# Linear attention: query sums halved by GpSimd, key copies on ScalarE, query round 1 earlier

## The reference

```python
# b = 32 images, C = 32 channels, n = 256 positions, heads = 4, dh = 32
xn = x / norm * g[None, :, None, None] * C ** 0.5
q, k, v = jnp.split(einsum('bchw,oc->bohw', xn, w_qkv), 3, axis=1)
k = concatenate([mk, k], axis=-1)      # 4 memory keys per head
v = concatenate([mv, v], axis=-1)      # and their values
q = softmax(q, axis=-2) * scale        # over the 32 channels of a head
k = softmax(k, axis=-1)                # over the positions
context = einsum('bhdn,bhen->bhde', k, v)
out = einsum('bhde,bhdn->bhen', context, q)
return einsum('bchw,oc->bohw', out, w_out) + b_out
```

## Time and profile before

| | us |
|---|---|
| median of 3 runs | 586.63 |
| lowest and highest | 584.84, 587.69 |
| profiled execution, its own time | 583.12 |
| its span | 581.3 |
| end of the linear attention stage in it | 84.41 |
| VectorE busy, whole span | 408.9 (70%) |
| TensorE busy, whole span | 504.9 (87%) |
| GpSimd busy, whole span | 158.7 (27%) |
| mean granted TensorE clock | 0.966 of full speed |

### The profile page before, as it was taken

How to read it: one execution, slowest core, us unless ns; L and a number is a source line. 1 busy time by engine, 2 the same in 40 slices (tenths; PEclk the granted TensorE clock), 3 DMA queues, 4 the chain that set the end, 5 groups by cost and what they waited for, 6 DMA issues and landing times. The chain is left out here.

```text
span 581.3 us, 15235 instructions
## 1 busy us (share of the span) xinstructions
PE 504.9 (87%) x6330; PEld 289.8 (50%) x6337; DVE 408.9 (70%) x766; ACT 303.6 (52%) x525; POOL 158.7 (27%) x210
## 2 busy tenths in 40 slices
PE   7856889998897989798898888899999999999993
PEld 3445654466655642365555534436543654365420
DVE  5669977775454799787889838866756584658463
ACT  3257544234342310359888844465656555656482
POOL 0116422000000000405666600002860386038500
PEclk9989899999999889999999979979999999999997
DMA  8400015000000381000000000000000000000002
GB/s 257 44 8 3 3 35 206 1 1 2 1 2 1 69 200 23 2 1 1 3 1 2 3 19 2 7 12 3 1 3 11 1 2 1 12 1 2 1 7 77
DMA packets 22560, 15.03 MB, mean 26 GB/s; under 512 B 17465, under 2 KB 20569, under 8 KB 22362
## 3 DMA queue, kind: packets, MB, share of 16 engines
q1 hardware_dynamic: 22490, 14.00, 9.7%
HBM read 8.71 MB, written 1.08 MB: 17 GB/s over the span
## 5 line engine op out<-in xcount | busy, mean ns | idle before, releaser
L2030 ACT ACTIVATE R<-ps 128x512 f32<-128x512 f32 x96 | 52.1, 594 | 41.5 <-PE ps L1743 41.5
L2205 DVE TENSOR_REDUCE R<-ps 128x4 f32<-128x1024 f32 x48 | 56.6, 1210 | 10.0 <-PE ps L1729 9.5
L2113 POOL TENSOR_TENSOR R<-R 128x512 f32<-128x512 f32 x42 | 53.3, 1268 | 15.3 <-ACT R L2030 15.2
L1519 POOL TENSOR_TENSOR R<-R 128x512 f32<-128x512 f32 x32 | 45.3, 1417 | 43.2 <-DVE R L1453 43.2
L1453 DVE TENSOR_TENSOR R<-ps,lasting 128x512 f32<-128x512 f32 x64 | 41.2, 685 | 11.7 <-PE ps L1379 11.7
L1743 PE MATMUL ps<-tmpA,R 32*128 32x256 f32 x384 | 49.3, 374 | 0.0
L1729 PE MATMUL ps<-R,tmpA 32*128 32x256 f32 x384 | 47.7, 400 | 0.0
L1486 ACT ACTIVATE R<-R 128x1536 f32<-128x1536 f32 x32 | 47.3, 1479 | 0.1
L1379 PE MATMUL ps<-R,Q 32*128 32x128 f32 (+1 forms) x512 | 29.9, 346 | 10.0 <-ACT R L1502 10.0
L1743 PEld LDWEIGHTS ps<-tmpA,R 32*128 32x128 f32 x384 | 36.2, 185 | 1.0
L1379 PEld LDWEIGHTS ps<-R,Q 32*128 32x128 f32 x512 | 23.9, 184 | 20.8 <-DVE R L1453 16.9
(11 more groups left out here) (323 smaller groups left out, 1082.9 us busy)
## 6 DMA issues: line engine op xcount, KB each, us to landing
R<-z SPq DMA_DIRECT2D x32, 128.0 KB, 2.4
R<-in_qv SPq DMA_DIRECT2D x1, 2560.0 KB
x<-in_x SPq DMA_DIRECT2D x4, 256.0 KB, 3.5
out<-x SPq DMA_DIRECT2D x4, 256.0 KB, 3.9
lasting<-in_lasting SPq DMA_DIRECT2D x1, 811.0 KB, 8.5
early<-in_early SPq DMA_DIRECT2D x1, 793.5 KB, 7.6
scatter<-in_scatter SPq DMA_DIRECT2D x1, 512.0 KB, 6.2
P<-scratch_w SPq DMA_DIRECT2D x16, 32.0 KB, 2.5
```

The lines of the kernel that those rows point to most:

```text
L1519: pool.tensor_tensor(diagonal(u), diagonal(u), diagonal(u), ALU.mult).then_inc(diag_squared[1], 1)
L2030: act.activation(m.et[:, g % 2, j, :], ps[:, turned_bank(g, j), :], ACT.Exp)\
L2113: pool.tensor_tensor(m.esum[:, g % 2, two, :], m.et[:, g % 2, two, 0:N], m.et[:, g % 2, two, N:2 * N], ALU.add).then_inc(sg["halves_added" ...
L2205: dve.tensor_reduce(m.parts[:, g % 2, :, a:a + 2, 3 * g].rearrange("p s i -> p i s"), ps[:, a:a + 2, :].rearrange("p i (s m) -> p i s m", ...
```

## The change

Four parts. The sums: GpSimd adds the upper 16 channels of each head to the lower 16 (`add_halves`, 128x256) into two alternating buffers in `m.z`, and VectorE's sum reads 16 instead of 32 values per head. GpSimd's list becomes: halves of unit u + 1, then the multiply of unit u. The copies: the turned key maxima and the memory term are copied by ScalarE instead of VectorE; the turning of the memory exponentials and its copy move ahead, beside the weight products of bank 7. TensorE's order: query round 1 goes ahead of key round 0, query round 2 ahead of key round 1, query round 3 from behind context(4, 8) to behind context(0, 4). The lists of VectorE and ScalarE follow: the sums of a round are taken one round later.

```diff
--- before.py
+++ after.py
@@ -216,8 +216,6 @@
     ones_set = sem("la_ones_set")
     memmax_ready = sem("la_memmax_ready")
     memexp_done = sem("la_memexp_done")
-    mem_ready = sem("la_mem_ready")
-    mem_copied = sem("la_mem_copied")
     w2mem_ready = sem("la_w2mem_ready")
     w2mem_copied = sem("la_w2mem_copied")
     kproj_ready = sem("la_kproj_ready")
@@ -236,6 +234,7 @@
     qmax_ready = sem("la_qmax_ready")
     qsub_done = sem("la_qsub_done")
     qexp_done = sem("la_qexp_done")
+    qhalves_added = sem("la_qhalves_added")
     qsum_ready = sem("la_qsum_ready")
     qinv_ready = sem("la_qinv_ready")
     qnorm_done = sem("la_qnorm_done")
@@ -271,6 +270,10 @@
 
     def q_stat(t, u):
         return t[:, 16 * u:16 * u + 16]
+
+    def q_halves(u):
+        at = 768 + u % 2 * 256
+        return m.z[:, at:at + 256].rearrange("p (j h d) -> p j h d", j=J, h=HEADS)
 
     BY_V = (11, 13, 15)
 
@@ -390,12 +393,14 @@
                     key_maxima(J * r + i)
 
             key_maxima_round(0)
+            pe.wait_ge(memexp_done, 1)
             pe.wait_ge(wo_spread, 1)
+            pe.transpose(ps[0:MEM, 7, 256:384], m.kem[:, :], m.ident[:, :])
             pe.matmul(ps[:, 7, 0:128], m.wvt[:, :], m.wobd[:, :], start=True, stop=True)
             pe.matmul(ps[0:MEM, 7, 128:256], m.memvt[:, :], m.wobd[:, :], start=True, stop=True).then_inc(wvo_ready, 1)
             pe.wait_ge(m.lasting_loaded, 16 * 2)
             key_maxima_round(1)
-            pe.wait_ge(wvo_made, 2)
+            pe.wait_ge(wvo_made, 3)
             value_round(0)
             key_maxima_round(2)
             key_maxima_round(3)
@@ -404,24 +409,21 @@
             query_round(0)
             value_round(2)
             value_round(3)
+            query_round(1)
             pe.wait_ge(parts, 4)
             pe.wait_ge(v_copied, UN)
             pe.transpose(ps[:, 4, 0:64].bitcast(BF16), m.kparts[:, :, :].rearrange("p j r -> p (j r)"),
                          m.identb[:, :]).then_inc(turned, 1)
-            pe.wait_ge(memexp_done, 1)
-            pe.transpose(ps[0:MEM, 5, 0:128], m.kem[:, :], m.ident[:, :]).then_inc(mem_ready, 1)
-            pe.wait_ge(mem_copied, 1)
             for h in range(HEADS):
-                mm = pe.matmul(ps[rows_of(h), 6, 0:33], m.kemt[:, rows_of(h)], m.memvo[:, h, :],
+                mm = pe.matmul(ps[rows_of(h), 5, 0:33], m.kemt[:, rows_of(h)], m.memvo[:, h, :],
                                start=True, stop=True)
             mm.then_inc(w2mem_ready, 1)
             pe.wait_ge(turned_copied, 1)
             pe.wait_ge(w2mem_copied, 1)
             key_round(0)
-            query_round(1)
+            query_round(2)
             key_round(1)
             key_round(2)
-            query_round(2)
             key_round(3)
             pe.wait_ge(ones_set, 1)
             pe.wait_ge(kexp_done, 2 * NCH)
@@ -429,7 +431,7 @@
             for u in range(0, 4):
                 query_transposes(u)
                 context(4 * u, 4 * u + 4)
-                if u == 1:
+                if u == 0:
                     query_round(3)
             for u in range(4, 8):
                 query_transposes(u)
@@ -491,6 +493,7 @@
                     dve.tensor_scalar(m.wvo[:, :], ps[:, 7, 0:128], m.gs[:, 0:1], None, ALU.mult).then_inc(wvo_made, 1)
                     dve.tensor_copy(m.memvo[:, :, 0:C], ps[0:MEM, 7, 128:256].rearrange("p (h c) -> p h c", h=HEADS))\
                         .then_inc(wvo_made, 1)
+                    dve.tensor_copy(m.kemt[:, :], ps[0:MEM, 7, 256:384]).then_inc(wvo_made, 1)
             dve.wait_ge(kmax_ready, UN)
             dve.tensor_scalar(m.kmax[:, :], m.kmax[:, :], m.small[:, 0:1], None, ALU.max).then_inc(km_ready, 1)
 
@@ -502,8 +505,8 @@
                                   ALU.subtract).then_inc(qsub_done, 1)
 
             def invert_sums(u):
-                dve.wait_ge(qexp_done, u + 1)
-                dve.tensor_reduce(by_head(q_stat(m.qsum, u)), q_unit(u), AXX, ALU.add).then_inc(qsum_ready, 1)
+                dve.wait_ge(qhalves_added, u + 1)
+                dve.tensor_reduce(by_head(q_stat(m.qsum, u)), q_halves(u), AXX, ALU.add).then_inc(qsum_ready, 1)
                 dve.wait_ge(qsum_ready, u + 1)
                 dve.reciprocal(q_stat(m.qinv, u), q_stat(m.qsum, u)).then_inc(qinv_ready, 1)
 
@@ -517,21 +520,16 @@
                 dve.wait_ge(q_ready, r + 1)
                 for i in range(RND):
                     subtract_maxima(RND * r + i)
-                    if r == NCH - 1 and i:
-                        invert_sums(RND * r + i - 1)
-                    if r == 0 and i == 2:
-                        dve.wait_ge(turned, 1)
-                        dve.tensor_copy(m.kmrow[:, :], ps[:, 4, 0:64].bitcast(BF16)).then_inc(turned_copied, 1)
-                        dve.wait_ge(mem_ready, 1)
-                        dve.tensor_copy(m.kemt[:, :], ps[0:MEM, 5, 0:128]).then_inc(mem_copied, 1)
-                        dve.wait_ge(w2mem_ready, 1)
-                        dve.tensor_copy(m.w2mem[:, :], ps[:, 6, 0:33]).then_inc(w2mem_copied, 1)
-                    if r == 2 and i == 2:
-                        dve.wait_ge(memterm, 2)
-                        sum_context(0)
-                for i in range(RND if r < NCH - 1 else 0):
-                    invert_sums(RND * r + i)
-            invert_sums(UN - 1)
+                    if r >= 2:
+                        invert_sums(RND * (r - 1) + i)
+                if r == 1:
+                    for u in range(RND):
+                        invert_sums(u)
+                if r == 2:
+                    dve.wait_ge(memterm, 2)
+                    sum_context(0)
+            for u in range(UN - RND, UN):
+                invert_sums(u)
 
             def copy_queries(u):
                 dve.wait_ge(qt_ready, u + 1)
@@ -591,6 +589,10 @@
                     copy_values(RND * r + i)
             act.wait_ge(km_ready, 1)
             act.activation(m.kfac[:, :], m.kmax[:, :], ACT.Exp, bias=m.small[:, 0:1], scale=-1.0).then_inc(f_done, 1)
+            act.wait_ge(turned, 1)
+            act.activation(m.kmrow[:, :], ps[:, 4, 0:64].bitcast(BF16), ACT.Copy).then_inc(turned_copied, 1)
+            act.wait_ge(w2mem_ready, 1)
+            act.activation(m.w2mem[:, :], ps[:, 5, 0:33], ACT.Copy).then_inc(w2mem_copied, 1)
             def key_round(r):
                 act.wait_ge(k_ready, r + 1)
                 for a in range(2):
@@ -599,18 +601,17 @@
             for u in range(RND):
                 query_exponentials(u)
             key_round(0)
+            for u in range(RND, 2 * RND):
+                query_exponentials(u)
             key_round(1)
-            for u in (4, 5, 6):
-                query_exponentials(u)
+            query_exponentials(8)
             key_round(2)
-            query_exponentials(7)
+            query_exponentials(9)
             key_round(3)
-            query_exponentials(8)
+            query_exponentials(10)
             copy_queries(0)
-            query_exponentials(9)
-            query_exponentials(10)
+            query_exponentials(11)
             copy_queries(1)
-            query_exponentials(11)
             copy_queries(2)
             for i in range(4):
                 query_exponentials(12 + i)
@@ -680,7 +681,17 @@
                                    .broadcast_to([128, G // 2, J, 33]),
                                    m.w2mem[:, None, None, :].broadcast_to([128, G // 2, J, 33]),
                                    ALU.mult).then_inc(memterm, 1)
+            def add_halves(u):
+                pool.wait_ge(qexp_done, u + 1)
+                if u >= 2:
+                    pool.wait_ge(qsum_ready, u - 1)
+                pool.tensor_tensor(q_halves(u), q_unit(u)[:, :, :, 0:DH // 2], q_unit(u)[:, :, :, DH // 2:DH],
+                                   ALU.add).then_inc(qhalves_added, 1)
+
+            add_halves(0)
             for u in range(UN):
+                if u + 1 < UN:
+                    add_halves(u + 1)
                 pool.wait_ge(qinv_ready, u + 1)
                 pool.tensor_tensor(q_unit(u), q_unit(u), by_head(q_stat(m.qinv, u)).unsqueeze(3)
                                    .broadcast_to([128, J, HEADS, DH]), ALU.mult).then_inc(qnorm_done, 1)
```

## The result

The changed kernel takes 592.62 us in the median of 15 executions, the kernel before 586.92 in 15 of its own; the ratio is 1.009, 95% interval 1.0056 to 1.0124. It is slower by 5.7 us where +1.0 was forecast.

What follows compares the result with a forecast made beforehand. Two chains bound the linear attention stage: key rounds with TensorE's list (+0.4 us) and VectorE's list (2.55 late less 1.54 slack, +1.0). The first lies under the second: 586.63 + 1.0 = 587.6 us, range 585.1 to 590.3.

Steps and rivals of the forecast that it cites:

- ScalarE's new order and its key rounds: Linear attention stage: four query exponentials go before key round 1's, nothing lost; its exponentials end at 51.2 us, as before.
- key round 1 is ready at 49.2: TensorE: third query round, after VectorE's unit 7 (46.4), ends at 47.6 us; key round 1 follows, ready at 49.2.
- Key round 3 ends at 58.65: ScalarE's last key exponentials end at 58.65 us against 58.25, +0.4 us on the chain of key rounds and TensorE's list.
- The rival: TensorE's clock stays low through key rounds 1 to 3, 2.8 instead of 1.6 us each: +4.6 us, 591.2; chance 0.12.
- the second query round fill the idle stretch near 40: TensorE runs the second query round from 39.4 to 41.0 us, ahead of the first key round.
- VectorE's unit 7: TensorE, working on the first key round until 45.2 us, then waits for VectorE to finish this unit at 46.4.
- The halves on GpSimd: GpSimd's 0.73 us adds make VectorE wait where sums follow one another; +1.0 us at the stage's end after slack.
- the two paced places: Sums 0 to 3 and sums 12 to 15, four in a row each, where VectorE waits for GpSimd.
- The forecast waits: VectorE waiting for GpSimd: about 2.5 us between 47 and 51 us, 3.5 between 70 and 76.
- VectorE's saving: Rival: VectorE gains 3.0 us from its wait and 3.7 from the sums, less 0.25: 6.4 us, 580.2; chance 0.08.
- the wait for query round 3: VectorE idles some 2.5 us after sum_context(0) at about 59 us, until 62.2, losing most of its gain.
- The early copy behind L492: VectorE's 4x128 copy of turned memory keys moves from 41.68 to 23.55 us; +0.25 us for everything behind.

Runs made afterwards that it cites:

- The kernel with four fillers: Changed kernel plus one unread 128x256 fp32 matmul in each key round, four in all, where TensorE waits: median 589.87 us, ratio 1.0068.
- fillers in the waits: Changed kernel plus unread matmuls where TensorE waits in the key rounds: twelve 128x512 bf16, median 591.70 us; four 128x256 fp32, median 589.87 us.
- split key rounds: Key rounds made in two halves of two banks: in the changed kernel median 591.71 us, ratio 1.0062; in the kernel before 588.90, ratio 1.0049.

## Why the prediction was wrong

**The step that failed** is the one on ScalarE's new order and its key rounds, with the walk from there on: "key round 1 is ready at 49.2" and "Key round 3 ends at 58.65", at 1.6 us each. It took the granted clock from the profiled execution of before and kept it. With the low clock, key rounds 1 to 3 take about 2.8 us each (their exponentials start 4.82 us apart, 1.94 of it on ScalarE). Key round 1 is ready at 51.9, its exponentials and those behind it end at 63.51, and query round 3 ends at 68.4 instead of 62.2. The rival had this with the right mechanism, 3 x 1.2 us, but a chance of 0.12. It was to decide from two such rounds on, and the profile has three. In the means it is 61.7 against 48.7 us of low clock, 0.32 us lost per us by the fit, so 4.2 of the 5.6 us.

**Why the rival's chance of 0.12 was too little.** The profiled execution of before was 3.5 us under the median, and I treated that as an offset. Most of it was the clock: mean 0.966 against 0.958 over 89 executions, 3.0 us by the slope. Low key rounds already occur in the kernel before, as its second profile shows. I also let the second query round fill the idle stretch near 40 and overlooked that TensorE then waits four times for about 2 us (2.36, 2.04, 2.07 and 2.16, where before had 0.72, 2.06, 0.95 and 2.15). The first of them, for VectorE's unit 7, I had taken as 1.2. That these waits keep the clock low is not shown.

**The halves on GpSimd** were right in mechanism and nearly in size. Forecast +1.0, measured +1.6 at the same clock (changed against before), by the fit. Taking them out gives 2.0 back, and taking out only the two paced places 1.6, with no wait for GpSimd left. The forecast waits were 2.5 and 3.5, measured 2.26 and 3.15. The add was 0.734 us for 0.73. Left out of the forecast was what a late VectorE does to the last transposes and the final products: TensorE waits 0.80 and 1.27 us for its copies, the clock falls, and the products take 1.3 us more, in all three profiles of the changed kernel and in neither of before. The kernel with four fillers, which has the halves too, shows no such stretch, so it does not follow from the halves alone.

**VectorE's saving** of 3.0 + 3.7 us did not arrive, as argued: it went into the wait for query round 3. Its size was forecast as 2.5 and was 7.9, mostly through the clock. (By the prediction's own times, 59 to 62.2 less the context sum, it should have read about 3; nothing else was worked out from it.) The early copy behind L492 took 0.27 us and set what follows back by 0.19 (0.25 taken), and the copies as a whole cost nothing that can be told from zero.

**The clock, as far as it goes.** That fillers in the waits remove 11 to 12 us of low clock (standard error 3) in an otherwise unchanged order is shown, with 12 and with 4 of them. That the new order raises it (57.7 against 50.1) is 2.7 standard errors, that the halves do (54.0 against 48.7) 2.4. What decides stays open: split key rounds took the same waits nearly away and left the low clock at 58.7, and in their profile it was low while TensorE was busy 14.58 of 16 us. The Trainium skill, "TensorE: Matmul & The Clock Gate", section "A second HAM failure mode: psum-queue depth-cycling", says of a bf16 kernel that cycles through PSUM banks that frequent short idles between groups of matmuls make the clock go up and down. The trace of the changed kernel agrees as far as the clock is low across waits of at most 2.2 us, but here it stayed low for 20.5 us, and with split key rounds it was low with only two waits, of 0.7 and 1.2 us.

## What to carry to other kernels

Before a forecast, ask which draw the profiled execution was: if it lies under the median and its granted clock above the mean, its fast stretches are not the kernel's. Where TensorE works in bursts with a clock that is low in part of them, price the work behind every moved round at both clock levels, and do not count on a filled wait to bring the clock back. And when a helper engine takes work from a busy one, walk the places where requests come back to back: at 1.73 us a unit GpSimd kept up with 1.93, and paced 0.60.

## What the runs showed of the hardware

- Executions of one program on one core spread over more than 10 us (580.4 to 594.7 for the kernel before), about three quarters of it with TensorE's mean granted clock, at 3.8 us for each 0.01.
- With twelve more matmuls TensorE's last instruction ended 3.2 us behind all other engines', over 500 us after the place where they were added; with four it did not (one profile each).
- Four extra 128x256 fp32 matmuls in waits brought the low clock from 61.7 to 49.9 us and cost 1.3 us on their own, by the fit.
- With split key rounds the clock stayed at 1.2 GHz for 27.3 us, though TensorE was busy 14.58 of 16 us in it, with weights of 32x128.
